# Attention: one product with ones on the sum of two key tiles' exponentials, where neither tile is masked

## The reference

```
qkv = x @ qkv_w.T + qkv_b            # x taken as (2, 1024, 512); 16 heads of 32
q, k = _rope(q), _rope(k)
scores = einsum('bhqd,bhkd->bhqk', q, k) / sqrt(32)
scores = where(causal, scores, -inf)
attn = softmax(scores, axis=-1)
out = einsum('bhqk,bhkd->bqhd', attn, v) @ out_w.T + out_b
```

## Time and profile before

| | |
|---|---|
| median of 3 executions | 1510.72 us (1508.88 to 1512.7) |
| profiled execution, its own time | 1510.53 us |
| its span | 1508.7 us |
| PE busy | 1458.7 us |
| DVE busy | 918.8 us |
| attention, from the first score product to the output projection | 904 to 1226 us |
| one middle unit | 39.2 us |

### The profile page before, as it was taken

How to read it: one execution, slowest core, us unless ns; L and a number is a source line. 1 busy time by engine, 2 the same in 40 slices (tenths; PEclk the granted TensorE clock), 3 DMA queues, 4 the chain that set the end, 5 groups by cost and what they waited for, 6 DMA issues and landing times. The chain is left out here.

```text
span 1508.7 us, 22471 instructions
## 1 busy us (share of the span) xinstructions
PE 1458.7 (97%) x7696; PEld 1077.8 (71%) x7696; DVE 918.8 (61%) x1833; ACT 621.4 (41%) x1095; POOL 545.0 (36%) x455
## 2 busy tenths in 40 slices
PE   7999989999999999999999999999999999999987
PEld 6788778788888888888888775555555457777554
DVE  6887887855544654554343566666666238667664
ACT  5343455613421441342122115665566636442544
POOL 1233233302430441242053223344446557104773
PEclk9999999999999999999999998999999999999999
DMA  6121447503320531232355787666664634844336
GB/s 218 33 63 63 159 161 247 195 19 126 97 84 0 167 97 42 84 97 91 128 178 176 225 249 192 184 188 178 191 185 188 221 139 173 315 187 136 103 103 240
DMA packets 105227, 223.38 MB, mean 148 GB/s; under 512 B 9328, under 2 KB 35312, under 8 KB 104240
## 3 DMA queue, kind: packets, MB, share of 16 engines
q1 hardware_dynamic: 101392, 211.96, 43.2%
q0 software_dynamic: 3744, 10.23, 2.2%
HBM read 157.54 MB, written 64.36 MB: 147 GB/s over the span
## 5 line engine op out<-in xcount | busy, mean ns | idle before, releaser
L969 POOL TENSOR_TENSOR ff_w_lo<-ff_raw,ff_w_hi 128x1024 fp32r<-128x1024 f32 x64 | 153.8, 2403 | 220.9 <-ACT ff_w_hi L999 206.7
L2039 ACT ACTIVATE at_pt<-at_st 128x512 f32<-128x512 f32 (+3 forms) x384 | 161.4, 507 | 94.2 <-PE at_st L2076 90.9
L115 PE MATMUL op_bank<-ff_x_hi,ff_w_lo 128*128 128x512 f32 x512 | 199.9, 390 | 0.2 <-issue 0.2
L116 PE MATMUL op_bank<-ff_x_lo,ff_w_hi 128*128 128x512 f32 x512 | 199.7, 390 | 0.0
L117 PE MATMUL op_bank<-ff_x_hi,ff_w_hi 128*128 128x512 f32 x512 | 199.6, 390 | 0.0
L1239 DVE TENSOR_TENSOR ff_h_lo<-ff_hf,ff_h_hi 128x512 f32 (+1 forms) x64 | 146.9, 2295 | 53.8 <-ACT ff_h_hi L1127 53.6
L1384 DVE CUSTOM_DVE_ANT_0 mx_mx<-mx_mx,mx_mask 128x128 f32<-128x128 f32 (+2 forms) x200 | 100.8, 519 | 28.3 <-PE mx_mx L1372 27.3
L999 ACT ACTIVATE ff_w_hi<-ff_raw 128x1024 fp32r<-128x1024 f32 x64 | 67.8, 1061 | 118.5 <-PE op_bank L117 116.1
L2076 PE MATMUL at_st<-mx_qp,mx_kp 98*128 98x512 f32 (+3 forms) x288 | 106.1, 391 | 7.5 <-ACT at_pt L2039 4.2
L115 PEld LDWEIGHTS op_bank<-ff_x_hi,ff_w_lo 128*128 128x128 f32 x512 | 96.5, 188 | 20.8 <-issue 0.6
L117 PEld LDWEIGHTS op_bank<-ff_x_hi,ff_w_hi 128*128 128x128 f32 x512 | 96.4, 188 | 20.2
(11 more groups left out here) (471 smaller groups left out, 3405.2 us busy)
## 6 DMA issues: line engine op xcount, KB each, us to landing
ff_raw<-in_Wug SPq DMA_DIRECT2D x64, 512.0 KB, 3.6
at_raw<-in_expert_gu SPq DMA_DIRECT2D x16, 704.0 KB, 12.3
mx_qp<-q_hi SPq DMA_DIRECT2D x12, 512.0 KB, 6.6
mx_kp<-k_hi SPq DMA_DIRECT2D x12, 512.0 KB, 10.8
at_raw<-in_expert_d SPq DMA_DIRECT2D x8, 768.0 KB, 13.9
expert_gu_bf<-at_cast SPq DMA_DIRECT2D x16, 352.0 KB, 11.3
ex_e_gu<-expert_gu_bf SPq DMA_DIRECT2D x8, 704.0 KB, 8.4
tm_ln_res<-in_x SPq DMA_DIRECT2D x4, 1024.0 KB, 5.4
```

Of the source, the lines that this page charges most:

```text
L115: pe.matmul(out, cut_l(ll), cut_r(rh), start=first, stop=False, **kw)
L116: pe.matmul(out, cut_l(lh), cut_r(rl), start=False, stop=False, **kw)
L969: pool.tensor_tensor(w[j][1][:, :, :, :], raw[:, j], f32(w[j][0][:, :, :, :]), ALU.subtract)\
L2039: act.activation(pt[:, s % PT, h, off:TB], st[(s * HG + h) % ST][:, off:TB], ACT.Exp, scale=SCALE).then_inc(exp_done, 1)
```

## The change

In an unmasked pair the quad of products with ones is no longer made for each of the two steps. DVE adds the two steps' exponentials (four heads by 512 queries, 2048 elements per partition) into a new tile `pt_sum`, and PE makes one quad with ones on that sum, behind the second step's values. Behind the sum on DVE stand the copy of `num` and the tops of the next pair. The sum of a pair waits until the quad that read the previous sum is done. To make room for `pt_sum`, `den_sb` loses its second buffer (ACT's copy of `den` then waits for the division before it instead of for a store), and the expert weights have two `raw` buffers in place of three. Two semaphores are merged.

```diff
-        num_sb, den_sb = b.sb("num_sb", [P, QC, TB]), b.sb("den_sb", [P, QC, TB])
+        num_sb, den_sb = b.sb("num_sb", [P, QC, TB]), b.sb("den_sb", [P, TB])
+        pt_sum = b.sb("pt_sum", [P, HG, TB])
...
+        def whole(steps):
+
+            return all(diag(s) is None for s in steps)
...
+        def last_whole(u, steps):
+
+            earlier_ones = [k + PAIR for k in range(0, steps[0], PAIR) if whole([k, k + 1])]
+            return earlier_ones[-1] if earlier_ones else max(k + PAIR for k in range(0, NS, PAIR) if whole([k, k + 1])) - NS
...
             def copy_den(u, qc):
                 act.wait_ge(pv_done, u * NS + ENDS[qc] + 1)
-                at_least(act, o_stored[qc], u * DMA)
-                act.activation(den_sb[:, qc, :], den[:, :], ACT.Copy).then_inc(copied, 1)
+                at_least(act, divided, (u * QC + qc) * DIVIDE_OPS)
+                act.activation(den_sb[:, :], den[:, :], ACT.Copy).then_inc(copied, 1)
...
+                pair = [s - s % PAIR, s - s % PAIR + 1]
                 for total, lhs in ((num, None), (den, ones)):
+                    if whole(pair) and lhs is not None:
+                        if s == pair[0]:
+                            continue
+                        pe.wait_ge(summed, u * WHOLE + wholes(pair[0]) + 1)
+                    moving = pt_sum if whole(pair) and lhs is not None else pt[:, s % PT]
...
                 if TURN_STEP in steps and u + 1 < UNITS:
                     mx.join(dve, u + 1)
+                if whole(steps):
+                    dve.wait_ge(exp_done, (u * NS + steps[-1] + 1) * HG)
+                    at_least(dve, pv_done, u * NS + last_whole(u, steps))
+                    dve.tensor_tensor(pt_sum[:, :, :], pt[:, steps[0] % PT, :, :], pt[:, steps[1] % PT, :, :], ALU.add).then_inc(summed, 1)
                 ended = ended_before(u, steps)
                 if ended:
                     copy_num(*ended)
...
-    BUFFERS = 3
+    BUFFERS, RAW = 3, 2
...
     def load(self, sp, n):
         e, g = self.pieces[n]
-        sp.wait_ge(self.narrowed, n - self.BUFFERS + 1) if n >= self.BUFFERS else None
+        at_least(sp, self.narrowed, n - self.RAW + 1)
```

More of the change, by code:

```diff
@@ L1879, in attend @@
         last_at = b.next_at() - 3 * TT * C * 4
-        num_sb, den_sb = b.sb("num_sb", [P, QC, TB]), b.sb("den_sb", [P, QC, TB])
+        num_sb, den_sb = b.sb("num_sb", [P, QC, TB]), b.sb("den_sb", [P, TB])
+        near = b.sb("near", [P, TB])
         ones = b.sb("ones", [P, HD])
-        near = b.sb("near", [P, TB])
+        pt_sum = b.sb("pt_sum", [P, HG, TB])
         st = [b.psum(f"st{s}", [P, TB]) for s in range(ST)]
@@ L1906, in diags @@
             return sum(diag(k) is not None for k in range(s))
+        STARTS = [s for s in range(NS) if STEPS[s][1] == 0]
         ENDS = [s for s in range(NS) if s == NS - 1 or STEPS[s + 1][0] != STEPS[s][0]]
@@ L1921, in pieces_at, with wholes @@
             return [(u + 2, n) for n in range(lo, hi)]
+        def whole(steps):
+            return all(diag(s) is None for s in steps)
+        WHOLE = sum(whole([s, s + 1]) for s in range(0, NS, PAIR))
+        def wholes(s):
+            return sum(whole([k, k + 1]) for k in range(0, s, PAIR))
+        def last_whole(u, steps):
+            earlier_ones = [k + PAIR for k in range(0, steps[0], PAIR) if whole([k, k + 1])]
+            return earlier_ones[-1] if earlier_ones else max(k + PAIR for k in range(0, NS, PAIR) if whole([k, k + 1])) - NS
         def pairs():
@@ L2028, in near_inverse @@
                 at_least(act, divided, n * DIVIDE_OPS)
-                act.activation(near[:, :], den_sb[:, qc, :], ACT.Ln).then_inc(near_ready, 1)
+                act.activation(near[:, :], den_sb[:, :], ACT.Ln).then_inc(near_ready, 1)
                 act.wait_ge(near_ready, 2 * n + 1)
@@ L2095, in pv @@
                         mm = pe.matmul(total[rows, off:TB], vv[u % SLOTS][:, kt, rows] if lhs is None else lhs[:, :],
-                                       pt[:, s % PT, h, off:TB], start=first, stop=last, skip_group_check=True)
+                                       moving[:, h, off:TB], start=first and (lhs is None or not whole(pair)) or lhs is not None and whole(pair) and pair[0] in STARTS, stop=last, skip_group_check=True)
                 mm.then_inc(pv_done, 1)
-            pe.wait_ge(ones_small_set, 1)
+            pe.wait_ge(mx.ones_set, SLOTS)
             before = None
@@ L2192, in __init__ @@
         self.a = a
-        self.raw = [b.sb(f"raw{s}", [P, NM * C]) for s in range(self.BUFFERS)]
+        self.raw = [b.sb(f"raw{s}", [P, NM * C]) for s in range(self.RAW)]
         self.cast = [b.sb(f"cast{s}", [P, NM * C], BF16) for s in range(self.BUFFERS)]
-        self.loaded = [b.sem(f"loaded{s}") for s in range(self.BUFFERS)]
+        self.loaded = [b.sem(f"loaded{s}") for s in range(self.RAW)]
         self.stored = [b.sem(f"stored{s}") for s in range(self.BUFFERS)]
```

23 lines of the change are left out of this document (12 added, 11 removed).

## The result

The changed kernel took **1544.55 us** (median of 4 runs, 1543.14 to 1545.34), the one before 1510.09 beside it: a ratio of 1.0223, 95% interval 1.0207 to 1.0239. It is slower, as forecast, but by 34.5 us where I had written 6.9, and far outside my range of 1508 to 1524. The profiled execution took 1545.13 us, its span 1543.4, at a mean granted clock of 0.973 (before 0.989).

What follows compares the result with a forecast made beforehand. PE, busy 97% of the span, was taken as the bound, with DVE full while PE makes scores. New waits of 8.8 us less 1.9 saved gave +6.9 on 1510.53, forecast 1517.6 us after a 0.2 median adjustment; range 1508 to 1524.

Steps and rivals of the forecast that it cites:

- the saving: On PE, four quads per pair become three: 0.86 us each, 1.72 us per unit in units 0 to 6.
- the first sum: DVE's 2.27 us sum of steps 4 and 5 makes step 6's first top and the seventh piece 1.56 us late.
- the second sum: DVE's sum of steps 6 and 7 delays step 8's first top 2.26 us and the eighth piece 2.11 us.
- the cast held by the sum: POOL's first expert cast waits for DVE's second sum to end at 1017.66; hidden from PE.
- the balance without the clock: Attention: 1.25 us more for each of seven units, 8.8, less 1.9 saved in the last unit: +6.9 us.
- the third load: Expert load behind the first cast takes 4.0 us; step 8's mask is done by 1025.2, before PE at 1026.74.
- the rival that DVE hides the sums: Sums cost PE nothing, but the mask takes back 0.7 us in five units: 1500.4 us; chance 0.09.
- The clock falls: Rival: PE's idle time after a sum halves its clock once per unit, 2.8 us each: 1537 us; chance 0.05.

Runs made afterwards that it cites:

- e8: Changed kernel, but from unit 1 on sums cover only 16 of 512 queries, and the third expert cast stands behind step 9's mask: 1509.56 us.
- e11: e8 with the last unit's quads as before the change: 1509.00 us.
- e4_pad: Changed kernel, with PE repeating a score product 5 times in step 6 and 7 times in step 8, where it would wait: 1523.44 us.
- e2: Changed kernel, but from unit 1 on DVE sums only 16 of the 512 queries: 1527.57 us.
- e1: Changed kernel without sums: one den_sb, two raw buffers and merged semaphores alone: 1514.33 us.
- e9: Changed kernel with each sum and its quad one pair later, third expert cast behind step 9's mask, last unit's quads as before: 1515.42 us.
- e13: e9 plus 5 repeated score products in step 8 and 4 in step 9, units 0 to 6: 1528.40 us.
- e16: e9 plus 5 repeated score products in step 10 and 3 in step 11, inside PE's waits, units 0 to 6: 1511.21 us.
- e17: e9 with only the sum of steps 6 and 7, plus 9 repeated products in step 10 and 2 in step 11: 1515.59 us.
- e10: e5 with the third expert cast late and the last unit unchanged: 1524.03 us.
- e5: Changed kernel with the quad on the sum made ahead of its pair's two value quads: 1518.86 us.
- e3: Changed kernel in which PE waits for the sums but still makes all quads with ones on pt: 1557.30 us.

## Why the prediction was wrong

**Right: the saving.** 1.72 us per unit forecast, 39.2 - 37.5 = 1.7 in e8 and e11.

**Right: the first sum.** 1.56 us late forecast, 1.50 measured. Additions of 2.27 us forecast, 2.29 the median of 16.

**Nearly right: the second sum.** Against the start of step 8's scores, the eighth piece was forecast 2.11 - 0.70 = 1.41 us late; it starts 5.21 us after them (at 1034.38, scores at 1029.17) against 3.41 before (1017.96 and 1014.55), 1.80 late. The sum itself took 2.58 us here, beside a cast of POOL. My forecast had the cast held by the sum, at no cost to PE; it was the sum that was held, as it started later. That is the same lock of the two engines, with the other one paying.

**Right: the balance without the clock.** +6.9 us forecast; e4_pad's attention is 6.5 us longer than before, its unit 40.7 us (forecast 40.4). That they agree to 0.4 us is partly luck: the seven units are 9.5 us longer (forecast 8.8), and the last one 3.0 shorter (forecast 1.9), where e4_pad has 3.4 us of half clock and the kernel before 6.8.

**Right in the changed kernel: the third load.** The timeline of POOL after:

```profile
1032.00 1.36 POOL L2241 CAST at_cast<-at_raw 128x1408 bf16<-128x1408 f32 x1 [2.19 <-DMA at_raw<-in_expert_gu]
1035.90 1.47 POOL L2241 CAST at_cast<-at_raw 128x1536 bf16<-128x1536 f32 x1 [2.54 <-DMA at_raw<-in_expert_d]
1037.32 1.22 POOL L2029 TENSOR_SCALAR_AFFINE_SELECT at_pt<-at_pt 128x512 f32<-128x512 f32 x2
```

The masks are done at 1038.5 and `pv` of step 8 starts at 1042.71, without a wait. But the load was undersized: from its issue at 1029.84 to the cast it takes 6.1 us, and 4.9 in e2 (1029.76 to 1034.66), not 4.0. In e1, where PE is on time, the mask does hold it, by up to 0.6 us; by my numbers (mask at 1024.5, PE at 1025.49) that was hidden. So the rival that DVE hides the sums would not have given 1500.4 us either. e2, which is that case, gave 1527.6, with the mask as the next wait and a fall of the clock behind it.

**Wrong: the clock.** The step that failed is the rival *The clock falls*: I gave it 0.05 and once per unit, 1537 us, and the argument against it was that "the scores around my waits carry pieces, so PE does much more work in them than in the last unit". The pieces did not protect it. In five of the seven units the clock fell behind both waits. Per unit it is 43.6 - 40.7 = 2.9 us, 3.3 in the middle unit, about what I had priced *one* fall at (2.8 us). Each fall was thus half as dear as I thought and came twice as often. The last unit, in which I had counted no fall beyond the one it had, adds 2.7 (45.9 us from its maxima to the first projection, 43.2 in e4_pad): seven times 3.0 and 2.7 are the 23.8. Some evidence was in my own rows: the wait of 1.01 us on PE in the last unit had half clock at its end. It was not all one way, though. The same unit has a second wait, of 0.97 us, ending at 1215.0, with full clock behind it, which I did not show. One of two is weak evidence, but it is more than 0.05. The reason that I set against it was an argument, not a row.

What stays open. (1) What besides the wait decides a fall: why the clock fell in e9 behind 0.26 and 0.21 us in some units and not in others, and held in e13 behind 1.27. (2) The spread: e16's 12 runs go from 1505.84 to 1517.83 us, with mean clocks from 0.992 down to 0.984. They are 12 us apart, and 0.008 of 1510 us is 12 us. Its scatter goes with the clock (in e17 less closely: 1514.12 us at 0.993, 1518.7 at 0.990), but what differs from run to run no trace of one execution tells. (3) Why unit 0 of e10 has a fall of twice the length of e5's. (4) A whole sum beside full protection of the last unit was not tried.

## What to carry to other kernels

When PE bounds a kernel, price a new wait on it twice: the wait, and the products that run at half clock behind it. Here two waits of 1.2 and 1.7 us per unit cost about their own length again. If a wait cannot be avoided, work put into it that nobody needs can pay (e4_pad: 12 products more per unit, 21 us less), but it has to stand exactly there: nine wider products two steps earlier (e13) kept the clock in the profile and cost 13 us in the median. And read PE's busy time against its count of products: fewer products with more busy time is the clock, not a wait.

## What the runs showed of the hardware

- TensorE's granted clock went from 1.00 to 0.51 some 1.7 us behind a wait of 1.16 us (changed kernel, 1022.31) in the midst of scores and pieces that had kept PE busy, and stayed low for 3 to 4 us. It does not always: e13 kept 1.00 behind a wait of 1.27 us, e3 behind three of 1.17.
- Falls came with waits of each kind: for tops of DVE, for a mask of POOL (2.00 us, quads of 1.94 us behind it in place of 1.06), for exponentials of ACT (1.01 us in the last unit, quads of 1.94). In the last two the clock was down before the wait ended.
- The Trainium skill, in "SBUF — State Buffer" (the section on the two separate sides), has a DVE operation with two SBUF inputs and a GpSimd operation that reads SBUF lock each other out; the trace agrees: in the changed kernel the sums take 2.29 us alone, and 2.58 and 3.49 where a cast had started just ahead; where the sum started first it took 2.29 and the cast up to 3.36, for 1.36 alone.
